# One transposing transfer of 2048 columns per chunk for both halves of the attention probabilities

## The reference

```python
q_r = jnp.einsum('bshq,hqr->bhsr', q_big, W_qr)
k_r = jnp.einsum('bld,hdr->bhlr', kv_r, W_kr)
scores = jnp.einsum('bhsr,bhlr->bhsl', q_r, k_r)
attn = jax.nn.softmax(scores, axis=-1)
ctx_c = jnp.einsum('bhsl,bld->bhsd', attn, kv_r)
ctx_lat = jnp.einsum('bhsd,hkd->bhsk', ctx_c, w_kc_kv)
```

## Time and profile before

| | |
|---|---|
| median of 3 executions | 1279.04 us (1278.4 to 1282.54) |
| span of the profiled execution, first to last instruction | 1277.9 us |
| PE / DVE / ACT / POOL busy, share of the span | 88% / 82% / 54% / 31% |
| attention loop, first to last transposing issue | 196.4 to 986.0 us |
| transposing transfers | 256 + 256, each 128 x 1024 float16 (256 KB) |
| data moved | 174.83 MB; 39.07 MB read from HBM |

### The profile page before, as it was taken

How to read it: one execution, slowest core, us unless ns; L and a number is a source line. 1 busy time by engine, 2 the same in 40 slices (tenths; PEclk the granted TensorE clock), 3 DMA queues, 4 the chain that set the end, 5 groups by cost and what they waited for, 6 DMA issues and landing times.

```text
span 1277.9 us, 26541 instructions
## 1 busy us (share of the span) xinstructions
PE 1127.8 (88%) x9080; PEld 841.0 (66%) x9080; DVE 1053.2 (82%) x1198; ACT 690.2 (54%) x1025; POOL 397.3 (31%) x369
## 2 busy tenths in 40 slices
PE   5999998999999999999999999999988876745588
PEld 3555557788878888887777787777756332314567
DVE  3887778999999899898888888888864599998943
ACT  1222237777777777787777777777762210112312
POOL 2992441343443222121222212212210455333300
PEclk9999999999999999999999999999999987977689
DMA  8443308999999999999999999999994200210000
GB/s 293 136 140 101 97 15 142 174 181 179 180 181 178 180 181 178 180 166 180 178 182 184 184 183 183 185 182 183 186 189 75 99 0 0 102 79 1 1 17 17
DMA packets 562111, 174.83 MB, mean 137 GB/s; under 512 B 543264, under 2 KB 549408, under 8 KB 561952
## 3 DMA queue, kind: packets, MB, share of 16 engines
q1 hardware_dynamic: 560464, 169.17, 65.9%
q10 hardware_dynamic: 1616, 5.24, 1.1%
HBM read 39.07 MB, written 1.05 MB: 31 GB/s over the span
## 4 chain that ended last, share of the span: by engine, by line
SPq 50%; PE 21%; issue 13%; DVE 11%; POOL 2%; DMA 2%; ACT 1%; DVEq 0%; POOLq 0%; ACTq 0%
SPq L328 24%; SPq L325 24%; PE ps_o L1084 3%; PE ps_s L1059 3%; PE ps_o L1188 2%; DVE prod L934 2%; POOL prod L486 2%; DVE mix L940 2%; PE ps_t L1046 1%; PE ps_t L1047 1%; PE ps_t L1048 1%; PE ps_o L1074 1%; DVE hT L977 1%; DVE mixo L953 1%; DVE prod L944 1%
## 5 line engine op out<-in xcount | busy, mean ns | idle before, releaser
L820 DVE SCALAR_TENSOR_TENSOR p_lo<-prob,p_hi 128x1024 f16<-128x1024 f32 x256 | 319.5, 1248 | 83.0 <-DMA pt_lo<-p_lo 63.3
L569 ACT ACTIVATE p_hi<-prob 128x1024 f16<-128x1024 f32 x256 | 270.7, 1058 | 148.2 <-DMA pt_hi<-p_hi 140.7
L576 ACT ACTIVATE prob<-ps_s,nmax 128x1024 f32<-128x1024 f32 x256 | 284.3, 1111 | 56.0 <-DVE nmax L827 53.8
L827 DVE TENSOR_REDUCE nmax<-ps_s 128x1 f32<-128x1024 f32 x256 | 311.1, 1215 | 0.5 <-PE ps_s L1140 0.3
L1151 PE MATMUL ps_o<-kn_hi,pt_hi 128*128 128x128 f16 x2048 | 259.5, 221 | 5.3 <-DMA pt_hi<-p_hi 4.7
L1152 PE MATMUL ps_o<-kn_lo,pt_hi 128*128 128x128 f16 x2048 | 257.0, 219 | 0.0
L1138 PE MATMUL ps_s<-kt_hi,q_hi 128*128 128x512 f32 x512 | 224.6, 439 | 24.3 <-ACT prob L576 21.7
L1151 PEld LDWEIGHTS ps_o<-kn_hi,pt_hi 128*128 128x128 f16 x2048 | 194.3, 98 | 75.1 <-issue 62.8
L434 POOL TENSOR_TENSOR osum<-oscl 128x256 f32<-128x256 f32 x64 | 47.2, 738 | 515.5 <-DVE oscl L856 515.5
L1140 PE MATMUL ps_s<-kt_hi,q_lo 128*128 128x512 f32 x512 | 202.3, 395 | 0.0
L1152 PEld LDWEIGHTS ps_o<-kn_lo,pt_hi 128*128 128x128 f16 x2048 | 201.4, 98 | 0.0
(11 more groups left out here) (109 smaller groups left out, 1518.7 us busy)
## 6 DMA issues: line engine op xcount, KB each, us to landing
wgu_raw<-w_gu_dram SPq DMA_DIRECT2D x11, 512.0 KB, 7.7
wq_s<-wq_t_dram SPq DMA_DIRECT2D x16, 256.0 KB, 3.6
wot_s<-wo_t_dram SPq DMA_DIRECT2D x16, 256.0 KB, 2.8
kvr<-ctx_kv_dram ACTq DMA_DIRECT2D x4, 1024.0 KB, 14.1
pt_hi<-p_hi SPq DMA_TRANSPOSE x256, 3.3
pt_lo<-p_lo SPq DMA_TRANSPOSE x256, 3.2
kvr<-w_mix_dram SPq DMA_DIRECT2D x16, 256.0 KB, 3.0
wkcq_s<-w_kcq_dram SPq DMA_DIRECT2D x16, 192.0 KB, 2.6
```

The source lines that it names most:

```text
L569: nc.scalar.mul(p_hi[:, j % 2, :], prob[:, j % 2, :], PSCALE).then_inc(hi_done, 1)
L576: nc.scalar.activation(prob[:, j % 2, :], ps_s[:, 2 * (j % 2):2 * (j % 2) + 2, :].rearrange("p a c -> p (a c)"), ACT.Exp, bias=nmax[:, i, ...
L820: nc.vector.scalar_tensor_tensor(out=p_lo[:, j % 2, :], in0=prob[:, j % 2, :], scalar=PSCALE, in1=p_hi[:, j % 2, :], op0=ALU.mult, op1=ALU ...
L827: nc.vector.tensor_reduce(nmax[:, i, c:c + 1], ps_s[:, 2 * (j % 2):2 * (j % 2) + 2, :].rearrange("p a c -> p (a c)"), AX_X, ALU.max, negat ...
```

## The change

The two float16 buffers become one, `p_both`, in which a row holds the 1024 high and then the 1024 low parts; the four slots of transposed tiles likewise become `pt_both`. The old names are views of these. SP no longer waits for `hi_done`. It waits for `lo_done` and issues one transposing transfer of 128 x 2048 float16. One semaphore pair, `pt_in`, replaces `hi_in` and `lo_in`. `take_hi` waits for it, `take_lo` now waits for `hi_done` alone, and `weighed_keys` waits for it once, ahead of its first matmul.

```diff
-                p_hi = sb(st, "p_hi", [P, 2, CHUNK], F16)
-                p_lo = sb(st, "p_lo", [P, 2, CHUNK], F16)
-                pt_hi = sb(st, "pt_hi", [P, 4, CHUNK // P, P], F16)
-                pt_lo = sb(st, "pt_lo", [P, 4, CHUNK // P, P], F16)
+                p_both = sb(st, "p_both", [P, 2, 2, CHUNK], F16)
+                pt_both = sb(st, "pt_both", [P, 4, 2, CHUNK // P, P], F16)
+                p_hi, p_lo = p_both[:, :, 0, :], p_both[:, :, 1, :]
+                pt_hi, pt_lo = pt_both[:, :, 0, :, :], pt_both[:, :, 1, :, :]
...
                 sp.wait_ge(pv_done, SPARE + n - 3)
                 sp.sem_inc(turn_go, 1)
-                sp.wait_ge(hi_done, SPARE + n + 1)
-                sp.sem_inc(turn_go, 1)
-                sp.dma_start(pt_hi[:, j % 4], p_hi[:, j % 2, :], transpose=True).then_inc(hi_in[j % 2], 16)
                 sp.wait_ge(lo_done, SPARE + n + 1)
                 sp.sem_inc(turn_go, 1)
-                sp.dma_start(pt_lo[:, j % 4], p_lo[:, j % 2, :], transpose=True).then_inc(lo_in[j % 2], 16)
+                sp.dma_start(pt_both[:, j % 4].rearrange("p a c q -> p (a c) q"),
+                             p_both[:, j % 2].rearrange("p a c -> p (a c)"),
+                             transpose=True).then_inc(pt_in[j % 2], 16)
...
             def take_hi(n, half, j):
 
-                act.wait_ge(hi_in[j % 2], 16 * SPARE + 16 * half)
+                act.wait_ge(pt_in[j % 2], 16 * SPARE + 16 * half)
                 act.wait_ge(exp_done, SPARE + n + 1)
...
-            def take_lo(n, half, j):
-
-                dve.wait_ge(lo_in[j % 2], 16 * SPARE + 16 * half)
+            def take_lo(n, j):
+
                 dve.wait_ge(hi_done, SPARE + n + 1)
...
-                pe.wait_ge(hi_in[j % 2], 16 * SPARE + 16 * (half + 1))
+                pe.wait_ge(pt_in[j % 2], 16 * SPARE + 16 * (half + 1))
...
-                pe.wait_ge(lo_in[j % 2], 16 * SPARE + 16 * (half + 1))
```

More of the change, by code:

```diff
@@ L218, in build @@
         turn_go = sem("turn_go")
-        hi_in = [sem(f"hi_in{i}") for i in range(2)]
-        lo_in = [sem(f"lo_in{i}") for i in range(2)]
+        pt_in = [sem(f"pt_in{i}") for i in range(2)]
         hi_done = sem("hi_done")
@@ L510, in _ @@
             for i in range(2):
-                act.sem_inc(hi_in[i], 16 * SPARE)
+                act.sem_inc(pt_in[i], 16 * SPARE)
             act.wait_ge(const_ok, 2)
@@ L730, in _ @@
                 dve.sem_inc(s, SPARE)
-            for i in range(2):
-                dve.sem_inc(lo_in[i], 16 * SPARE)
             def q_rope(h, i):
@@ L900, in head @@
                         row_maximum(t0 + j // NCH, j // NCH)
-                    take_lo(n0 + j, (b * H + h) * (NSTEP // 2) + j // 2, j)
+                    take_lo(n0 + j, j)
                     if last and b < B - 1 and j in KEY_STEPS:
```

## The result

| | before | changed |
|---|---|---|
| median | 1279.64 us (1278.4 to 1282.54, 4 executions) | 1393.81 us (1388.31 to 1396.0, 4 executions) |
| span of the profiled execution | 1277.9 us | 1394.2 us |

The changed kernel is slower by 8.84% (ratio 1.0884, 95% interval 1.0862 to 1.0906). The forecast was 1390 us.

What follows compares the result with a forecast made beforehand. SP's two transposing issues were taken as the bound. After merging, 254 intervals x 3.44 = 873.8 us against 767.8 (+106), +4 delays, +1 first issue: span 1389, median 1390 us; main case 1307 to 1428, 8 in 10 1305 to 1470.

Steps and rivals of the forecast that it cites:

- The bound before: SP's queue in the loop of the kernel before: its two transposing issues bound it, 2.86 us per chunk against PE's 2.78.
- The ring: take_hi, take_lo, issue, landing, next take_hi on the same slot: 6.88 us for two chunks, 3.44 per chunk.
- link 1: From the start of take_hi to the start of take_lo: 1.16 us.
- link 2: From the start of take_lo to SP's issue of the transfer: 1.31 us.
- link 3: From issue to landing and the next take_hi on that slot: 3.18 us before, 4.41 us with the longer stream.
- The delays: Beside the loop's ring: one-off delays that stay in part, +4 us, and a first issue later by one take_lo, +1.
- SP's issue: The merged transposing issue on SP, taken as proportional to columns: 2.46 us, with 1.23 us as lower end.
- Data after the whole issue: Rival at the merged transfer: data waits for the issue's end, link 3 5.52, 1532 us; 0.13 shared with other slower cases.
- Cheap issue and short ring: Rival at link 3: cheap merged issue, link 3 3.29, ring 5.76, interval 2.88 us, 1243 us in all; chance 0.08.
- PE's clock: Rival in the loop: PE's clock falls in its new idle gaps, +644, over 1900 us; chance 1 in 50.

Runs made afterwards that it cites:

- the better version: The changed kernel with four slots for p_both in place of two, merged transfer kept, last w_mix pieces loaded after the loop: 1236.61 us, ratio 0.967.
- the kernel with four transfers: The kernel before with each transposing transfer cut in two of 512 columns, so four per chunk, waits as before: 1915.77 us, ratio 1.4956.
- the kernel with the late high issue: The kernel before with SP waiting for lo_done ahead of both transposing issues, still two transfers of 1024 columns: 1314.3 us, ratio 1.0272.

## Why the prediction was right, and which step of it was not

**The bound before.** Right. With the slots taken out of play the two issues still set the time (1273.75 us), and taking one issue away then gains 37 us. The prediction never weighed one other candidate: the DMA engines were 97% busy in the loop. They were not the bound, since with the same four slots the merged transfer moves the same bytes 37 us faster than two.

**The ring.** Right in mechanism, and shown from four sides: closing it with two transfers (1432.67), opening it with slots (1236.61), shortening its stream by a quarter (1306.61) and by half (1240.45). The turn shown above was 6.66 us where 6.88 were forecast: link 1 was 1.09 for 1.16, link 2 was 1.32 for 1.31, link 3 was 4.25 for 4.41. Link 3 was too long because the 3.18 us had been read at a place where another transfer was still in flight; the minimum of 3.0 in the earlier trace rows plus 1.23 gives 4.23. The whole turn is 0.22 us shorter, 0.11 per chunk, worth 254 x 0.11 = 28 us less.

**The delays.** Too small. I added 5 us. Between the first and the last `take_hi`, at 197.2 and 1094.9 us, lie 897.7 us; without one interval of 18.5 us in the last head, 254 of them have a mean of 3.46 us. Over 3.33 that is 33 us. The two errors cancel almost wholly, and that is luck: the 1390 is better than its parts.

Most of the delays lie in the links of the ring and not beside it. Taken from the starts and landings in the trace over the first 245 turns, up to the last head, `take_hi` starts 0.02 us after the landing that it waits for in 242. The mean turn is 6.88 us, 0.22 more than the one shown, or 27 of the 33 us over 254 chunks. The mean of link 1 is 1.12, of link 2 1.41, of link 3 4.35 us. In link 2 `take_lo` itself lasts 1.28 us on average and up to 1.96, where 1.23 was read, and SP issues 0.03 us later than usual; in link 3 the landing comes after 4.32 us on average. The line of `take_lo`, min/median/max in ns:

```profile
L815 DVE SCALAR_TENSOR_TENSOR p_both<-prob,p_both x256: 1205/1225/1956, 198.3 to 1096.0; 128x1024 f16<-128x1024 f32 x128
```

**SP's issue.** Wrong: "proportional to columns, 2 x 1.23 = 2.46 us". The median was 1.86. The stream and the issue of 1024 columns last the same 1.23 us, and I took that for one process. They are two. The median issue is 1.23 to 1.33 us for 1024 columns and 1.25 to 1.26 for 512, then 1.43 for 1536 and 1.86 for 2048. The shortest ones show the fixed part best: 1.188, 1.231, 1.274 and 1.316 us at 512, 1024, 1536 and 2048 columns, 0.043 us more for each 512. What the larger ones take beyond that varies from issue to issue. The stream does grow with the columns. In the changed kernel the first issue runs from 199.61 for 2.03 us, and its data, in the two stretches below (columns as in the loop stretch above), begins about 200.9 and goes on past the end of the issue at 201.64:

```profile
199.60:200.80 1.20, 1.20 (x6) 0.92 (x6) 1.20 (x2) 1.02 (x2) 0.00 (x0) 1.00 0.00 0
200.80:203.20 2.40, 1.49 (x7) 1.02 (x6) 2.28 (x3) 1.09 (x2) 1.07 (x2) 1.00 1.07 198
```

The time came out right all the same, because link 3 rests on the stream's length and not on the issue's, and the stream did double. The error matters for the better version: with SP at 2.76 us per chunk it would stand level with PE's 2.78 even with an open ring, while in truth the merging frees about 0.6 us of SP per chunk and leaves PE the bound alone.

Of the two rules that the prediction weighed, the proportional issue, which it had drawn from one push per tile, is not borne out at these sizes, since 512 and 1024 columns cost the same. The other is the advice of the Trainium skill, "DMA: Bandwidth & Descriptors", section "Rules for kernel authors", to coalesce many small transfers into a large one. It holds for SP's issue here, 1.86 us for one against 2.49 for two, and turned to loss only by the ring.

**The rivals.** Data after the whole issue: excluded by the rows just shown. Cheap issue and short ring: half true, the issue was cheap and the ring long. PE's clock: stayed at 1.00 in the changed kernel. It did fall, to a mean of 0.89, in the kernel with four transfers, whose PE idles a third of the loop:

```profile
230.00:1600.00 1370.00, 904.04 (x7436) 683.86 (x7437) 654.74 (x873) 545.86 (x809) 147.25 (x267) 0.89 0.49 98
```

**What stays open.** Why the issue varies beyond 1024 columns (1.32 to 1.9 us and more at 2048), why `take_lo` and the landing are slower in some turns, and how the near bounds add up to 3.16 us per chunk in the kernel with the late high issue.

## What to carry to other kernels

When two transfers are merged, look at what the first one released: if a slot's refill waits for the merged landing, walk the ring refill, issue, landing and divide it by the number of slots. A merge that relieves a busy queue pays only with enough slots to keep that ring under the next bound; here four in place of two turned +114 us into -43 us. An issue time that equals the data time at one size proves nothing about how either scales; one run at another size does.

## What the runs showed of the hardware

- A transposing transfer between SBUF buffers (128 partitions, float16) costs SP a median of 1.25 to 1.26 us to issue at 512 columns, 1.23 to 1.33 at 1024, 1.43 at 1536 and 1.86 to 1.92 at 2048. The shortest issues differ by 0.043 us per 512 columns only.
- Its median landing after the start of the issue was 2.5, 3.0, 3.6 and 4.2 us at 512, 1024 (sent alone), 1536 and 2048 columns. The first three from the pages of those runs:

```profile
pt_hi<-p_hi SPq DMA_TRANSPOSE x512, 2.5
pt_hi<-p_hi SPq DMA_TRANSPOSE x256, 3.0
pt_both<-p_both SPq DMA_TRANSPOSE x256, 3.6
```

From the ends, 2.47 and 4.25 us, that is some 1.9 us and 0.59 us per 512 columns, or 128 KB at about 220 GB/s. The Trainium skill, "DMA: Bandwidth & Descriptors", section "Latency and other measured facts", gives 261 GB/s for a transposing transfer with a non-contiguous middle dimension and about 350 to 400 for a contiguous one. These runs stay below both.
